# Handing attention's turned output to the shared block through DRAM, with two buffers for each split part

## The reference

```python
def cond(x, mask, Wq, Wo):                    # x: (16, 256, 512)
    q = transpose(x) @ Wq.T                   # heads of 32
    scores = scale * q @ q.T                  # masked by column, then by row
    out = softmax(logits) @ q @ Wo.T
    return transpose(out)                     # (16, 256, 512)

def ffn(h):                                   # h: 4096 rows of 512
    shared = silu(h @ shared_gate_w) * (h @ shared_up_w) @ shared_down_w
    top_val, top_idx = top_k(h @ router_w, 2) # probs = sigmoid(top_val)
    return shared + sum over the chosen e of down_w[e](silu(gate) * up), gate, up = (prob * h) @ gate_up_w[e]

out = x + ffn(cond(x, cond_2048, Wq, Wo))
```

## Time and profile before

| | us |
|---|---|
| median of 3 runs | 1297.12 (1297.02 to 1301.38) |
| the profiled execution | 1294.72 |
| its span in the trace | 1292.6 |
| attention | 0 to about 669.7 |
| shared block | 669.9 to about 837 |
| experts | about 837 to the end |

### The profile page before, as it was taken

How to read it: one execution, slowest core, us unless ns; L and a number is a source line. 1 busy time by engine, 2 the same in 40 slices (tenths; PEclk the granted TensorE clock), 3 DMA queues, 4 the chain that set the end, 5 groups by cost and what they waited for, 6 DMA issues and landing times. The chain is left out here.

```text
span 1292.6 us, 21019 instructions
## 1 busy us (share of the span) xinstructions
PE 1210.9 (94%) x5500; PEld 665.1 (51%) x5501; DVE 700.9 (54%) x1243; ACT 490.9 (38%) x922; POOL 782.8 (61%) x526
## 2 busy tenths in 40 slices
PE   5999999999999999999969999789999999999995
PEld 2445544455444555545438999644444444444442
DVE  4676676676676776667415643334444444333333
ACT  1465566665656565656623222111111111111110
POOL 1587787787787787788850277235455544544443
PEclk8799999999999999999978999989999999999997
DMA  6566657657657656656323995344445555555651
GB/s 183 153 169 181 191 161 186 166 157 185 184 153 192 168 157 184 189 155 169 103 96 132 339 350 169 122 136 137 148 155 167 163 180 174 188 181 193 193 204 51
DMA packets 116493, 221.89 MB, mean 172 GB/s; under 512 B 18975, under 2 KB 21791, under 8 KB 116449
## 3 DMA queue, kind: packets, MB, share of 16 engines
q1 hardware_dynamic: 84960, 151.96, 40.3%
q0 software_dynamic: 23936, 54.72, 14.1%
q10 hardware_dynamic: 7552, 14.68, 3.6%
HBM read 150.14 MB, written 90.00 MB: 186 GB/s over the span
## 5 line engine op out<-in xcount | busy, mean ns | idle before, releaser
L746 DVE TENSOR_REDUCE row_max<-bank 128x1 f32<-128x512 f32 x512 | 343.5, 684 | 174.3 <-PE bank L568 173.8
L681 ACT ACTIVATE probsT<-bank 128x512 f32<-128x512 f32 x512 | 300.3, 596 | 227.3 <-PE bank L580 225.2
L437 POOL TENSOR_TENSOR key_sum<-key_sum,probsT 128x1024 f32<-128x1024 f32 x128 | 299.6, 2373 | 0.4 <-ACT probsT L681 0.4
L568 PE MATMUL bank<-k_stack,q_stack 96*128 96x512 f32 x512 | 282.2, 555 | 10.5 <-DMA q_stack<-q_hi 5.3
L1509 PE MATMUL bank<-gate_up_sb,rows_T 128*128 x576 | 273.0, 597 | 1.6 <-ACT rows_T L1456 1.6
L433 POOL TENSOR_TENSOR key_sum<-probsT 128x1024 f32<-128x1024 f32 x64 | 151.3, 2375 | 128.6 <-ACT probsT L681 128.6
L580 PE MATMUL bank<-q_stack,k_stack 99*128 99x512 f32 x512 | 207.0, 405 | 1.7 <-ACT probsT L681 1.5
L1374 POOL DMA_INDIRECT out<-rows_final,slot_info x72 | 73.1, 1015 | 186.6 <-DVE rows_final L1432 138.2
L568 PEld LDWEIGHTS bank<-k_stack,q_stack 96*128 96x128 f32 x512 | 98.5, 193 | 166.1 <-DVE row_max L746 126.9
L1463 ACT ACTIVATE gated<-bank 128x256 f32<-128x256 f32 x72 | 27.7, 384 | 359.1 <-PE bank L1509 359.1
L1509 PEld LDWEIGHTS bank<-gate_up_sb,rows_T 128*128 128x128 f32 x576 | 104.5, 192 | 106.4 <-issue 106.4
(11 more groups left out here) (141 smaller groups left out, 1406.3 us busy)
## 6 DMA issues: line engine op xcount, KB each, us to landing
expert_rows_dram<-zero_rows SPq DMA_DIRECT2D x16, 1152.0 KB, 7.2
expert_rows_dram<-rows_out SPq DMA_DIRECT2D x72, 256.0 KB, 2.4
k_stack<-hi_dram SPq DMA_DIRECT2D x60, 256.0 KB, 6.3
q_stack<-hi_dram SPq DMA_DIRECT2D x60, 256.0 KB, 7.1
x_row<-in_x SPq DMA_DIRECT2D x16, 512.0 KB, 3.5
rows_ext_dram<-hid SPq DMA_DIRECT2D x16, 512.0 KB, 5.7
tok<-rows_ext_dram SPq DMA_DIRECT2D x16, 512.0 KB, 7.9
x_in<-in_x SPq DMA_DIRECT2D x16, 512.0 KB, 7.4
```

Of the source, the lines that this page charges most:

```text
L437: nc.gpsimd.tensor_tensor(total, total, probs(k), ALU.add).then_inc(added, 1)
L568: nc.tensor.matmul(logit_bank[i % 2][:, :], q_stack[par][g][0:K_LOGIT, h, q * P:(q + 1) * P], k_stack[par][g][0:K_LOGIT, h, :], start=True ...
L681: nc.scalar.activation(probsT[:, j, :], key_bank[j % 2][:, :], ACT.Exp, scale=SCALE).then_inc(probs_ready, 1)
L746: nc.vector.tensor_reduce(row_max[g][:, i:i + 1], logit_bank[i % 2][:, :], AX.X, ALU.max)\
```

## The change

Attention stores hidT as well, into a new tensor `hidT_dram`, one DMA of 512 KB for each batch, with 4 KB in a row for each partition. hidT's layout changes so that this row is [KT, D]; ScalarE writes it with a stride and TensorE reads it for the router as before. Before it overwrites hidT, ScalarE waits for the last store (`turned_stored`). The shared block loads tok from hidT_dram, already turned. turn_tokens goes, and the hi and lo parts are made from tok in SBUF and not from a bank. Each part has two buffers, and batch b+2's parts are made after batch b's sh parts. TensorE waits for them in halves, inside gate_up. The count matmuls get a bank of their own and stand behind gate_up(1).

```diff
+        hidT_dram = nc.dram_tensor("hidT_dram", [B, P, KT, D], F32)
...
-        hidT = sb("hidT", [P, KD, KT, P])
+        hidT = sb("hidT", [P, KT, KD, P])
...
+            def store_turned(b, copied):
+                for name, count in copied:
+                    sp.wait_ge(emptied[BANK_OF[name]], count + 1)
+                    passed()
+                sp.dma_start(hidT_dram[bass.ds(b, 1), :, :, :].rearrange("o p k d -> p (o k d)"),
+                             hidT[:, :, :, :].rearrange("p k e c -> p (k e c)")).then_inc(turned_stored, 16)
...
                     if exists(kind, g, 3):
                         store_split(*place(b, par, g, 3), 1)
+                    if g == 1 and kind != FIRST:
+                        store_turned(b - 1, [(name, misc_count(b, kind, name)) for name in ("prev_hidT0", "prev_hidT1")])
...
             store_hidden(B - 1, [(name, tail(name)) for name in ("tail_hid0", "tail_hid1")])
+            store_turned(B - 1, [(name, tail(name)) for name in ("tail_hidT0", "tail_hidT1")])
             sp.wait_ge(hidden_stored, 16 * B + 16)
+            sp.wait_ge(turned_stored, 16 * B + 16)
             sp.wait_ge(rows_cleared, 16 * B)
...
-                        empty(name, c, hidT[:, int(name[-1]), :, :], four)
+                        act.wait_ge(turned_stored, 16 * b)
+                        empty(name, c, hidT[:, :, int(name[-1]), :], four)
...
-            tok = [rb(f"tok{i}", [P, KD, T]) for i in range(3)]
+            tok = [rb(f"tok{i}", [P, KT, D]) for i in range(3)]
             x_in = fb("x_in", [P, KD, T])
-            tokT_hi = rb("tokT_hi", [P, KT, D], F32R)
-            tokT_lo = rb("tokT_lo", [P, KT, D], F32R)
+            tok_hi = fb("tok_hi", [P, KT, D], F32R)
+            tok_lo = fb("tok_lo", [P, KT, D], F32R)
...
-                        sp.wait_ge(tok_turned, 2 * (b - 2))
-                    sp.dma_start(tok[i][:, :, :], rows_ext[b * D:(b + 1) * D, 0, :].rearrange("(k p) t -> p k t", p=P))\
+                        sp.wait_ge(tok_lo_ready, 2 * (b - 2))
+                    sp.dma_start(tok[i][:, :, :], hidT_dram[b, :, :, :])\
...
-                def turn_tokens(b):
-                    i = b % 3
-                    pe.wait_ge(tok_loaded[i], 16 * (b // 3 + 1))
-                    for h in range(2):
-                        if b >= 1:
-                            pe.wait_ge(tokT_lo_ready, 2 * b - 1 + h)
-                        for k in range(2):
-                            for m in range(KD):
-                                c = k * D + m * P
-                                last = nc.tensor.transpose(turn_bank[h][:, c:c + P],
-                                                           tok[i][:, m, (2 * h + k) * P:(2 * h + k + 1) * P], ident[:, :])
-                        last.then_inc(tok_turned, 1)
 
                 def gate_up(b):
                     i = b % 2
-                    pe.wait_ge(tokT_lo_ready, 2 * b + 2)
                     if b >= 2:
                         pe.wait_ge(sh_done, b - 1)
                     for hi, lo, dst in zip(shared_in_hi, shared_in_lo, (gate_bank[i], up_bank[i])):
                         for m in range(KI):
-                            last = products(dst[:, m * D:(m + 1) * D],
-                                            [(w[:, k, m * P:(m + 1) * P], t[:, k, :])
-                                             for k in range(KT) for w, t in ((hi, tokT_hi), (hi, tokT_lo), (lo, tokT_hi))])
+                            cols = slice(m * P, (m + 1) * P)
+                            for k in range(KT):
+                                if m == 0 and k % 2 == 0:
+                                    pe.wait_ge(tok_lo_ready, 2 * b + k // 2 + 1)
+                                t_hi, t_lo = tok_hi[i][:, k, :], tok_lo[i][:, k, :]
+                                last = products(dst[:, m * D:(m + 1) * D],
+                                                ((hi[:, k, cols], t_hi), (hi[:, k, cols], t_lo), (lo[:, k, cols], t_hi)),
+                                                k == 0, k == KT - 1)
                     last.then_inc(up_done, 1)
 
                 def down(b):
@@ -1068,36 +1074,28 @@
 
                     pe.wait_ge(constants_ready, 3)
                     pe.wait_ge(both_ready, 1)
-                    pe.wait_ge(tokT_lo_ready, 4)
                     flat = both[:, :, :].rearrange("p t e -> p (t e)")
-                    nc.tensor.matmul(turn_bank[0][:, 0:TT * E], earlier[:, :], flat, start=True, stop=True)
-                    nc.tensor.matmul(turn_bank[0][:, TT * E:2 * TT * E], ones[:, :], flat, start=True, stop=True)\
+                    nc.tensor.matmul(count_bank[:, 0:TT * E], earlier[:, :], flat, start=True, stop=True)
+                    nc.tensor.matmul(count_bank[:, TT * E:2 * TT * E], ones[:, :], flat, start=True, stop=True)\
                         .then_inc(counted, 1)
 
-                turn_tokens(0)
                 for b in range(B):
+                    gate_up(b)
                     if b == 1:
                         count_rows()
-                    elif b + 1 < B:
-                        turn_tokens(b + 1)
-                    gate_up(b)
-                    if b == 1:
-                        pe.wait_ge(counts_copied, 2)
-                        turn_tokens(2)
                     if b >= 1:
                         down(b - 1)
                 down(B - 1)
...
-                def copy_tokens(b):
+                def upper_tokens(b):
+                    act.wait_ge(tok_loaded[b % 3], 16 * (b // 3 + 1))
                     for h in range(2):
-                        act.wait_ge(tok_turned, 2 * b + h + 1)
-                        if h == 0 and b >= 1:
-                            act.wait_ge(up_done, b)
-                        nc.scalar.activation(tokT_hi[:, 2 * h:2 * h + 2, :],
-                                             turn_bank[h][:, :].rearrange("p (k c) -> p k c", k=2), ACT.Copy)\
-                            .then_inc(tokT_hi_ready, 1)
+                        if h == 0 and b >= 2:
+                            act.wait_ge(up_done, b - 1)
+                        nc.scalar.activation(tok_hi[b % 2][:, 2 * h:2 * h + 2, :], tok[b % 3][:, 2 * h:2 * h + 2, :], ACT.Copy)\
+                            .then_inc(tok_hi_ready, 1)
...
-                copy_tokens(0)
+                upper_tokens(0)
+                upper_tokens(1)
                 for b in range(B):
                     if b == 1:
                         act.wait_ge(best_ready, 1)
                         nc.scalar.activation(sigm[:, :, :], best[:, :, :], ACT.Exp, scale=-1.0).then_inc(sigm_ready, 1)
-                    if b + 1 < B:
-                        copy_tokens(b + 1)
                     silu(b)
                     upper_sh(b)
+                    if b + 2 < B:
+                        upper_tokens(b + 2)
...
-                        dve.wait_ge(tokT_hi_ready, 2 * b + h + 1)
-                        if h == 0 and b >= 1:
-                            dve.wait_ge(up_done, b)
-                        part = tokT_hi[:, 2 * h:2 * h + 2, :]
-                        v.tensor_tensor(tokT_lo[:, 2 * h:2 * h + 2, :],
-                                        turn_bank[h][:, :].rearrange("p (k c) -> p k c", k=2),
-                                        part.bitcast(F32), ALU.subtract).then_inc(tokT_lo_ready, 1)
+                        dve.wait_ge(tok_hi_ready, 2 * b + h + 1)
+                        part = tok_hi[b % 2][:, 2 * h:2 * h + 2, :]
+                        v.tensor_tensor(tok_lo[b % 2][:, 2 * h:2 * h + 2, :], tok[b % 3][:, 2 * h:2 * h + 2, :],
+                                        part.bitcast(F32), ALU.subtract).then_inc(tok_lo_ready, 1)
...
                 lower_tokens(0)
+                lower_tokens(1)
                 dve.wait_ge(constants_ready, 3)
                 choose(0, logits_all)
                 choose_second()
                 for b in range(B):
-                    if b + 1 < B:
-                        lower_tokens(b + 1)
                     combine(b)
                     lower_sh(b)
+                    if b + 2 < B:
+                        lower_tokens(b + 2)
```

22 lines of the change are left out of this document (12 added, 10 removed).

## The result

| | before | after |
|---|---|---|
| median of the runs, us | 1298.10 (4 runs, 1297.02 to 1301.38) | 1279.59 (4 runs, 1277.65 to 1281.65) |
| the profiled execution, us | 1294.72 | 1280.32 |
| its span in the trace, us | 1292.6 | 1278.2 |

The changed kernel takes 0.9857 of the time of the kernel before, 95% interval 0.984 to 0.9874. Beside a second set of twelve runs of before it was 0.9872 (0.9857 to 0.9888). The forecast of 1279.2 us was met to 0.4 us; the parts of it less well, as will be seen.

What follows compares the result with a forecast made beforehand. TensorE's own work was taken to bound the shared block. 7.1 us at its start plus 10.8 us of steady turns give 17.9, so 1297.1 - 17.9 = 1279.2 us; forecast 1277 to 1282 (chance 0.70), wider range 1276 to 1286.

Steps and rivals of the forecast that it cites:

- Steady turns: Shared block, gate_up(2) to the end of gate_up(15): twelve groups of 8 turns leave TensorE, 12 x 0.90 = 10.8 us gained.
- The seam: Start of the shared block: the first tok load waits for hidT's last store and goes 1.1 us later.
- Behind the load: First shared steps: gate_up(0) starts 1.8 us earlier, takes 7.6 us partly at half clock; gate_up(2) starts 7.1 us earlier.
- The second buffer: Shared block's start: batch 1 is split during gate_up(0), so gate_up(1) follows without the pause; part of the 7.1 us.
- Attention: Sixteen added 512 KB stores of hidT find room in the queue and nobody waits for them: cost 0.
- The sum: Shared block: 7.1 us at its start plus 10.8 us of steady turns, 17.9 us gained by the end of gate_up(15).
- Rival 1: Shared steps 1 to 8: DMA becomes the bound at 343 GB/s, steps 9.17 us, gain 11.7, 1285.4 us; chance 0.12.
- Rival 2: Shared block's end: GpSimd's 64 index scatters become the end, gain 14.5 to 17.9, at worst 1282.6 us; chance 0.08.
- Rivals 3 and 4: The first of the two: hidT's store delays attention's max rows, 42 us lost, 1321 us; chance 0.03.
- Rival 4: Shared steps: in-order engines hand a late token load on, TensorE pauses, two thirds of the gain gone, 1291 us; chance 0.05.

Runs made afterwards that it cites:

- two_buffers_old_order: Changed kernel with its two buffers, but batch b+1's parts made ahead of silu(b) and combine(b), as in the kernel before: 1278.94 us, 0.9863 of before.
- warm: Changed kernel plus 24 transposes of the identity before gate_up(0), to raise TensorE's clock: 1277.28 us, 0.9855 of before.
- two_buffers_only: Kernel before with two buffers for each split part, turns and plain rows kept: 1291.69 us, 0.9967 of before.
- one_buffer: Changed kernel with one buffer for each split part, in the changed order: 1336.09 us, 1.0305 of before.
- store_only: Kernel before with hidT's store, its layout and its wait added, nothing read from it: 1299.12 us, 1.0029 of before.
- more_dma: Changed kernel with every tok load issued twice, the first into a spare tile nothing reads: 1281.12 us, 0.9877 of before.
- one_buffer_old_order: Changed kernel with one buffer per split part and b+1's parts made ahead of silu(b) and combine(b): 1282.48 us, 0.9887 of before.

## Why the prediction came out right, point by point

**Steady turns, 10.8 us.** Right. From gate_up(2) to the last store it was 133.2 us and is 122.25 (695.91 to 818.16), 10.95 less. Copies from SBUF and their subtractions are covered, as two_buffers_old_order and the single wait for tok_lo show.

**The seam, 1.1 us later.** The mechanism is right, the size is not: 2.4 us. The mis-sized term is the landing of hidT's last store, taken at hid's 2.8 and measured at 3.9. Over the nine traces in which the block begins by waiting for that store it was 2.6 three times (seam 5.07 or 5.08, so 1.2 more than before) and 3.5 to 3.9 six times (seam 5.99 to 6.55). So the value I took occurs, but is the rarer one. It was within the bounds of 0.1 to 4.0. What makes a landing short or long I don't know.

**Behind the load.** Right to a few tenths: load to gate_up(0) 5.5 us predicted and 5.50 measured; gate_up(0) to gate_up(1) 7.6 and 7.42 (679.24 to 686.66); gate_up(0) to gate_up(2) 16.9 and 16.67. So gate_up(2) starts at 695.91, not 693.4, for the 1.4 us of attention and the 1.3 of the seam. The low clock costs one stretch. The prediction had 4.4 us of it and 4.4 x 0.45 = 2.0 us for it; it lasted 3.8 us (679.2 to 683.0), and warm, where gate_up(0) takes 5.74 us, puts the price at 1.7.

**The second buffer.** Its price as a part of before, 4.2 us, is what two_buffers_only shows. But the prediction gives it one role, to let gate_up(1) follow at once. It has another that I missed: the new order of ScalarE's and VectorE's queues works only with it. The forecast did not need this; the expectation for one_buffer did, and failed.

**Attention, 0.** Not contradicted. The load of max rows still lands in 1.8 us at the median and 2.7 at most. The 1.40 us in the trace of after are within the movement from run to run. store_only's median leaves up to 4 us for the store as a whole, of which the seam explains 1.2. What the remainder is stays open.

**The sum.** Between hid's last copy and the last store the prediction had 17.9 us, and the trace has 16.95. The missing 1.3 in the seam were partly made good by small terms behind it. The median fell by 18.5, the profiled execution by 14.4. That the forecast lies within 0.4 us of the median is in part luck: the movement of single runs is larger than that, and the drop against before is 18.5 us in one set of runs and 16.0 in the other.

**Rival 1 (DMA).** Fell. The steps are 8.40 us, and the queue gives 376 to 380 GB/s where 375 are wanted. The reading of 343 at share 1.03 as a ceiling is what is wrong with it, as more_dma shows. The Trainium skill (DMA: Bandwidth & Descriptors, Where 436 GB/s comes from) puts the HBM side of a core at about 358 GB/s, which it gets by halving what two cores share. The run of more_dma, with one core at work, passed that for 60 us at 401, and the measurement decides.

**Rival 2 (scatters).** Its mechanism holds, its price does not arise. The scatter of 729.70 began beside tok_lo, 1.36 us instead of 0.97, and ended at 731.06, 0.84 behind the first of the two subtractions (729.53 + 0.69): so it gets in between two in a row. That was the milder of the two forms: from the first scatter to the end of the last it is 82.9 us (726.94 to 809.88), where the prediction had 83.0 for this form (724.4 to 807.4) and 88.6 for the other. (Its start of 724.4 is 0.2 early by its own terms: 733.5 less 8.9 is 724.6.) The Trainium skill (SBUF — State Buffer, Who interferes with whom) has it that a VectorE instruction with two SBUF inputs contends with a GpSimd instruction that reads SBUF. The trace agrees, and shows that the scatter is held up for one such instruction and not for the row of them: the longest of the 64 took 1.36 us. A scatter's landing is 1.2 us, below the bounds I had.

**Rivals 3 and 4** did not come: no wait for max rows, no late loads. Rival 4's mechanism, a late wait that holds the queues behind it, is real; one_buffer is that case, though what came late there was a buffer and not a token load, and it is worse than I priced it, since it ends slower than before.

## What to carry to other kernels

Before moving a producer to another place in an in-order queue, write down for each instruction behind it what it now waits for at one remove: a second buffer can be what makes the order possible rather than a gain of its own, and taking it away here turned a gain of 1.3% into a loss of 3%. A full DMA share is not a bandwidth: shares of 1.03, 1.00 and 1.05 stood beside 343, 358 and 401 GB/s, so a rate read in one kernel is a demand until something is seen to wait for it. Where a block ends with a store that the next one has to wait for, bound its landing by all stores of its shape and not by the one nearest, and expect single executions to move by as much as such a term.

## What the runs showed of the hardware

- **A pause does not have a fixed price in clock.** In one_buffer TensorE pauses for 2.80 us before down in step after step. Behind the pause that ends at 745.93 the clock stays at its upper level (2.4 GHz); behind the one that ends at 757.37, of the same length, it falls to the lower (1.2 GHz). The windows behind the two:

```profile
745.90:746.90 1.00, 0.97 (x4) 0.86 (x5) 0.96 (x3) 0.00 (x0) 0.00 (x0) 1.00 1.05 408
746.90:748.00 1.10, 1.10 (x6) 0.88 (x5) 0.96 (x7) 0.00 (x0) 0.00 (x0) 1.00 0.92 339
...
757.40:758.40 1.00, 1.00 (x3) 0.78 (x4) 1.00 (x2) 0.00 (x0) 0.70 (x2) 0.70 1.02 389
758.40:760.00 1.60, 1.60 (x5) 1.28 (x4) 1.47 (x4) 0.03 (x1) 1.30 (x2) 0.50 1.02 391
```

  The first of these steps took 11.14 us from sgate to sgate, the second 13.0. Pauses of 1.51 us in one_buffer_old_order and 1.50 in one_buffer, before gate_up(1), cost no clock; two of 2.16 us (before, store_only) did.
- **The same 512 KB store lands in 2.6 or in 3.5 to 3.9 us** at the same quiet place, from execution to execution: the last store of hidT in three traces and in eight, with nothing between. The last store of hid, as large and issued 1.9 us earlier, took 2.7 or 2.8 us in all thirteen traces.
- **A core's DMA held 401 GB/s for 60 us**, in more_dma, with HBM reads and writes mixed; before had moved 343 at nearly the same share of busy engines. The share counts engines that have something in hand, and says little of what they could still take.
